# Router logits as columns of the output projection, and expert weights loaded in the last state-space block

## The reference

```python
h = tok(x)                                # patches -> LayerNorm -> W_proj -> LayerNorm, + positions
h = concatenate([h, txt(x_txt, ids)], 1)  # features of tokens -> LayerNorm -> gelu MLP
h = h + attn(layernorm(h))                # state-space block
h = h + ffn(layernorm(h))                 # mixture of 8 experts, one per token

def attn(x):                              # (32 sequences, 325 tokens, 192)
    xn = gamma * x / rms(x)
    xc = causal_conv4(xn @ W_in.T + b_in)             # 384 channels
    y  = scan(h = sigA * h + sigB * xc; y = h . sigC) # 16 states per channel
    return y @ W_out.T + b_out + x
def ffn(x):
    logits = x @ Ws + bs                  # 8 experts
    e = argmax(logits); p = max(softmax(logits))
    return (gelu(x @ W1[e] + b1[e]) @ W2[e] + b2[e]) * p
```

## Time and profile before

| what | us |
|---|---|
| median of 3 runs (lowest, highest) | 1399.47 (1394.68, 1400.88) |
| the profiled execution | 1397.25 |
| its span in the profile | 1395.5 |

### The profile page before, as it was taken

The page is one execution under the profiler, slowest core; times in us unless marked ns, Lnnn a source line. Parts: engine busy times, 40 slices in busy tenths (PEclk is TensorE's granted clock), DMA queues, the critical chain, the costliest instruction groups (busy, mean ns, idle before and its releaser), DMA issues. The chain is left out here.

```text
span 1395.5 us, 38297 instructions
## 1 busy us (share of the span) xinstructions
PE 1165.6 (84%) x11847; PEld 1099.6 (79%) x11847; DVE 808.4 (58%) x2553; ACT 690.4 (49%) x1544; POOL 389.3 (28%) x358
## 2 busy tenths in 40 slices
PE   0398993466579999999999679996699999999998
PEld 0398993244469898898898479985699999999998
DVE  0777977774752633633635547877456565655564
ACT  2265661255662332332233246654477777777775
POOL 6877000000200300300202105546233323333333
PEclk9999997576689998998999989998799999999999
DMA  8866412003510422322334489993111111111110
GB/s 186 183 99 146 105 36 66 26 0 99 233 26 2 105 67 79 79 82 72 71 96 100 122 252 293 304 286 100 54 47 43 46 41 44 46 45 43 45 43 24
DMA packets 166427, 133.83 MB, mean 96 GB/s; under 512 B 77989, under 2 KB 155932, under 8 KB 164704
## 3 DMA queue, kind: packets, MB, share of 16 engines
q1 hardware_dynamic: 152352, 112.22, 30.1%
q0 software_dynamic: 10384, 17.49, 4.0%
q10 hardware_dynamic: 3600, 3.01, 0.8%
HBM read 89.97 MB, written 43.53 MB: 96 GB/s over the span
## 5 line engine op out<-in xcount | busy, mean ns | idle before, releaser
L2126 POOL DMA_INDIRECT out_dram<-ob,oi x89 | 126.8, 1425 | 285.1 <-DVE ob L2180 279.9
L2236 PE MATMUL ph<-zt,wc 64*128 64x128 f32 x3204 | 197.8, 275 | 3.4 <-issue 1.6
L2236 PEld LDWEIGHTS ph<-zt,wc 64*128 64x128 f32 x3204 | 192.2, 189 | 6.8 <-issue 5.3
L2228 PE MATMUL py<-w2c,ht 64*128 64x192 f32 x2136 | 194.1, 327 | 1.1 <-DVE yb L2178 1.1
L1493 PE MATMUL pa<-wi,xn 96*85 (+3 forms) x2048 | 187.1, 247 | 2.9 <-POOL mc L1345 2.9
L1493 PEld LDWEIGHTS pa<-wi,xn 96*85 96x85 f32 (+1 forms) x2048 | 181.7, 156 | 4.1 <-POOL mc L1345 3.2
L2151 ACT ACTIVATE ht<-ph,bc 128x128 f32<-128x128 f32 x534 | 156.9, 371 | 48.5 <-PE ph L2236 48.5
L2228 PEld LDWEIGHTS py<-w2c,ht 64*128 64x128 f32 x2136 | 172.7, 187 | 1.5 <-issue 1.3
L1356 POOL TENSOR_TENSOR bd<-rr,mc 128x656 f32<-128x656 f32 x48 | 61.6, 1284 | 309.2 <-PE pb L1511 188.3
L1367 DVE COPY x<-pa 85x384 f32<-85x384 f32 x100 | 55.4, 554 | 147.2 <-PE pa L1493 147.2
L336 PE MATMUL ps_y<-wg,xt 128*112 128x192 f32 x672 | 123.0, 335 | 14.7 <-DVE yg L426 10.6
(11 more groups left out here) (318 smaller groups left out, 1964.9 us busy)
## 6 DMA issues: line engine op xcount, KB each, us to landing
y<-yd SPq DMA_DIRECT2D x41, 384.0 KB, 5.0
gp<-kd SPq DMA_DIRECT2D x48, 246.0 KB, 2.8
xg<-in_x SPq DMA_DIRECT2D x16, 588.0 KB
xr<-xs SPq DMA_DIRECT2D x89, 98.0 KB, 1.9
yd<-yt SPq DMA_DIRECT2D x56, 144.0 KB, 1.9
hb<-h SPq DMA_DIRECT2D x41, 192.0 KB, 5.9
yd<-yt SPq DMA_DIRECT2D x40, 192.0 KB, 2.1
xg<-in_x SPq DMA_DIRECT2D x48, 112.0 KB
```

The source lines that it names most:

```text
L2126: pool.indirect_dma_start(out, bass.IndirectOffsetOnAxis(ap=oi[j][:, 0:1], axis=0), ob[j][:], None, bounds_check=bound, oob_is_err=False). ...
L2228: m = pe.matmul(py[h][:], ht[j][r, k, :], w2c[j % 2][r, k, :], start=(k == 0), stop=(k == FC - 1))
L2236: return pe.matmul(ph[c % 4][:, c // 4, :], wc[j][r, f:f + 128], zt[j][r, part, :], start=start, stop=stop, skip_group_check=True)
```

## The change

- **Logits.** The router's weights, centred over the 192 features (`wsc`), are multiplied in the text stage with W_out and with its bias: 8 more columns of `wo` (200 instead of 192) and a row of `wi`. The projection then has 8 columns more and one more matmul per column, which adds bias and bias logits from one row of ones; the add of `bo` on DVE is gone, as are `turn`, `take` and `logits`. The residual's part of the logits is computed in `mix`: block 0's X units become H units with 104 columns, whose 8 logit columns go to `lgx`, and two L units transpose these into `lgh`; DVE scales `lgh` once and adds it per pair.
- **Expert weights.** Loaded by SP in the last block of `mix`, one expert behind each of the loads of g = 3 to 10, into the memory of `xn`, whose last use is over by then.
- **Buffers.** Four result banks and four row buffers. POOL, after the scatters of a group, waits for those of the group before.
- **Last group.** Ten columns in place of eight and two. The statistics of its columns 6 and 7 are not issued: `stats(LAST, FL, PG)` covers columns 8 and 9 only.
- **Images.** The last 8 stores move to the text stage's SP stream, and `root_y(g, 0, CUT)` behind the first of the last two `take`s.

```diff
@@ embed_images
             for g in range(NGRP):
+                hi = GRID if g + 1 < NGRP else CUT
+                sp.wait_ge(row_done, GRID * g + hi)
+                store_rows(sp, h0, keep, g, 0, hi)
...
-                if g + 1 == NGRP:
-                    root_y(g, 0, CUT)
                 for j in range(2):
                     take(g * GRID + GRID - 2 + j, j)
+                    if g + 1 == NGRP and j == 0:
+                        root_y(g, 0, CUT)
@@ embed_text, SP
+                sp.dma_start(wsc[:, n, :], io["L0_ffn_Ws"][n * HD:(n + 1) * HD, :]).then_inc(p_in, 16)
+            with nc.allow_non_contiguous_dma(reason="one value per partition"):
+                sp.dma_start(boc[:], io["L0_attn_b_out"].rearrange("(k p) -> p k", p=HD)).then_inc(p_in, 16)
+            sp.dma_start(wi[HD:HD + 1, 0, 0:D], io["L0_attn_b_out"].unsqueeze(0)).then_inc(p_in, 16)
+            store_rows(sp, dr["h0"], keep, NGRP - 1, CUT, GRID)
@@ embed_text, DVE
+            dve.wait_ge(p_turned, 1)
+            dve.scalar_tensor_tensor(out=wsc[:], in0=po[0][0:HD, 0, 0:NEX].unsqueeze(1).to_broadcast([HD, 2, NEX]),
+                                     scalar=-1.0 / D, in1=wsc[:], op0=ALU.mult, op1=ALU.add).then_inc(w2_ready, 1)
@@ embed_text, ACT
+                if m == 2:
+                    act.wait_ge(p_turned, 6)
+                    act.wait_ge(p_taken, 4)
+                    act.copy(wo[:, :, D:DX], po[1][:, 0, 0:KO * NEX].rearrange("p (k e) -> p k e", e=NEX))
+                    act.copy(wi[HD:HD + 1, 0, D:DX], po[1][HD:HD + 1, 1, 0:NEX]).then_inc(p_taken, 1)
+                    act.copy(wi[0:HD, :, EB:EB + NEX], wsc[:])
@@ embed_text, PE
+                if m == 2:
+                    pe.wait_ge(w2_ready, 1)
+                    for k in range(KO):
+                        for q in range(2):
+                            pe.matmul(po[1][:, 0, k * NEX:(k + 1) * NEX], wout_row[:, q, k * 128:(k + 1) * 128],
+                                      wsc[:, q, :], start=(q == 0), stop=(q == 1))
+                    for q in range(2):
+                        t = pe.matmul(po[1][0:HD + 1, 1, 0:NEX], boc[:, q:q + 1].to_broadcast([HD, HD + 1]), wsc[:, q, :],
+                                      start=(q == 0), stop=(q == 1))
+                    t.then_inc(p_turned, 1)
+                    pe.wait_ge(p_taken, 5)
@@ mix, SP
             def body(k, last):
                 for g in range(3, NG):
                     load(k, g, start(k) + 2 * (g - 2))
+                    if last and g - 3 < NEX:
+                        expert_weights(g - 3)
@@ mix, readers
+            if kind == "H":
+                flat = p[0:W, :, :].rearrange("w a b -> w (a b)")[:, 0:4 * (EB + NEX)].rearrange("w (c e) -> w e c", c=4)
+                copy(lgx[:, :, 4 * n:4 * n + 4], flat[:, EB:, :])
+                copy(x[:, :, 4 * n:4 * n + 4], flat[:, 0:EB, :]).then_inc(free[who], 1)
+            elif kind == "L":
+                copy(keep["lgh"][:, 4 * n:4 * n + 4, :], p[:, :, HALO:W]).then_inc(free[who], 1)
@@ mix, PE
             for m in range(XU):
-                input_unit(0, 0, m, m)
+                head_unit(m)
+            for n in range(LU):
+                p = bank(0, XU + n)
+                for who in range(2):
+                    pe.wait_ge(free[who], XU // 2 + 2)
+                for i in range(NEX // LU):
+                    tr = pe.transpose(p[:, i, 0:W], lgx[:, n * NEX // LU + i, :], ident[0:W, 0:W])
+                tr.then_inc(unit, 1)
@@ project_route, POOL
+            def group(g, a, half):
                 pool.wait_ge(rows_ok, g + 2)
                 hold(pool, tick_p)
+                scatter(a % NR, range(TG), a % 2)
+                if a:
+                    pool.wait_ge(sent[(a - 1) % 2], 16 * TG * (half + 1))
                     hold(pool, row_free)
@@ project_route, PE
             def project(p, g, q):
                 pe.wait_ge(y_in[q], 32 * (g + 1))
-                pe.wait_ge(h_done, p + 3)
+                pe.wait_ge(h_done, p + 1)
                 for i in range(2):
                     for k in range(KO):
+                        pe.matmul(po[q][:, i, 0:DX], yt[q][:, k, 1 - i, :], keep["wo"][:, k, :],
+                                  start=(k == 0), stop=False)
+                    m = pe.matmul(po[q][:, i, 0:DX], keep["ident"][0:HD + 1, HD:HD + 1].to_broadcast([HD + 1, CB]),
+                                  keep["wi"][0:HD + 1, 0, 0:DX], start=False, stop=True)
                 m.then_inc(out_ok, 1)
...
             def body(g, par, first):
                 for q in range(PG):
+                    project(PG * g + q, g, q)
                     if q == 2 and not first:
                         rank(g - 1, TG)
@@ project_route, DVE
                 dve.wait_ge(hb_ok, p + 1)
-                tt(hb[q][:], hb[q][:], bo[:, :].unsqueeze(1).to_broadcast([CB, 2, D]), ALU.add).then_inc(biased, 1)
-                dve.wait_ge(biased, p + 1)
                 dve.wait_ge(out_ok, p + 1)
...
+                tt(lgs[par][:, t:t + 2, :], po[q][:, :, D:DX], lgh[:, :, bass.ds(2 * p, 2)].rearrange("c e t -> c t e"),
+                   ALU.add)
+                tt(row[par][:, t:t + 2, 0:D], hb[q][:], po[q][:, :, 0:D], ALU.add).then_inc(h_done, 1)
...
+            dve.wait_ge(w_in, 32)
+            groups(dve, body, take_b1)
+            finish(NFULL, FL, 0, TG)
             c = Chain()
+            route1(LAST, FL, TL, stats(LAST, FL, PG), c)
+            route2(LAST, FL, TL, TG * LAST, mask10, c)
+            route3(LAST, FL, TL, TG * LAST, c)
```

More of the change, by code:

```diff
@@ L59 @@
 ROW = D + 4
+DX = D + NEX
 FAR = 1 << 20
@@ L854, in _ @@
             sums(0, HB)
-            pe.wait_ge(p_in, 80)
+            pe.wait_ge(p_in, 160)
+            for k in range(2):
+                t = pe.matmul(po[0][0:HD, 0, 0:NEX], keep["ones"][0:HD, 0:HD], wsc[:, k, :], start=(k == 0), stop=(k == 1))
+            t.then_inc(p_turned, 1)
             for k in range(2):
@@ L1226 @@
 XU = CB // 4
+LU = 2
 IU = EB // 4
@@ L1243, in unit_order, with mix @@
     return order
-def mix(nc, io, dr, keep, xn):
+def mix(nc, io, dr, keep, late, xn):
     with ExitStack() as ctx:
@@ L1493, in input_unit, with head_unit @@
                         mm = pe.matmul(p[:, i * EB:(i + 1) * EB], xn[0:rows, f, b, c * Q:c * Q + W],
-                                       keep["wi"][0:rows, f, bass.ds(k * EB, EB)],
+                                       keep["wi"][0:rows, f, bass.ds(k * EB + NEX, EB)],
                                        start=(f == 0), stop=(f == 1))
+                mm.then_inc(unit, 1)
+            def head_unit(m):
+                p = bank(0, m)[0:W, :, :].rearrange("w a b -> w (a b)")
+                for c in range(NCHUNK):
+                    for f in range(2):
+                        rows = HD + f
+                        mm = pe.matmul(p[:, c * (EB + NEX):(c + 1) * (EB + NEX)], xn[0:rows, f, m, c * Q:c * Q + W],
+                                       keep["wi"][0:rows, f, 0:EB + NEX], start=(f == 0), stop=(f == 1))
                 mm.then_inc(unit, 1)
@@ L1671, in project_route, with groups @@
         mu, rs = keep["mu"], keep["rs"]
-        w1, w2, b1, b2 = late["w1"], late["w2"], late["b1"], late["b2"]
-        def groups(eng, body):
+        b1, b2 = late["b1"], late["b2"]
+        def groups(eng, body, between=None):
             body(0, 0, True)
-            with eng.Fori(0, NFULL // 3) as i:
-                for a in range(1, 4):
-                    body(3 * i + a, a % 3, False)
+            if between:
+                between()
+            body(1, 1, False)
+            with eng.Fori(0, NFULL // NR) as i:
+                for a in range(2, 2 + NR):
+                    body(NR * i + a, a % NR, False)
         def empty_rows(eng, experts):
@@ L1793, in body @@
                     residual(g, q)
-                    if not (first and q == 0):
-                        take(PG * g + q - 1, (q - 1) % 2)
                     if not first and q == 0:
```

304 lines of the change are left out of this document (124 added, 180 removed).

## The result

The changed kernel takes 1435.54 us (median of 5, 1427.88 to 1436.55) against 1395.17 us for the kernel before on the same chip (median of 5, 1394.02 to 1400.88): ratio 1.0274, 95% interval 1.0249 to 1.0299. It is 2.7% slower. The forecast was 1401 us, with a range of 1387 to 1414.

What follows compares the result with a forecast made beforehand. Routing was taken as bound by a loop of DVE sums, PE's rank and projections (14.24 us a group), not PE alone. Terms summed to +2.4 us on 1397.25, giving 1399.7, or 1401.9 by the median; stated 1401, range 1387 to 1414.

Steps and rivals of the forecast that it cites:

- Images: Image stage: eight of SP's last 16 stores moved to the text stage, square root one copy later; -6.9 us.
- Text: Text stage: extra small matmuls, transfers and copies for the logit weights; +2.7 us.
- Inputs and L units: Inputs of block 0: records of 104 columns for 96, +3.4 us; two transpose units and a second drain, +2.0.
- Expert weights in the last block: Last state-space block: 9.44 MB between gp loads on SP's in-order queue delay gp; +14 us, bounds +10 and +25.
- rival 1: Last block starves: weights at 240 GB/s or below, block costs +25 us, total 1412; chance 0.25.
- in-order queue: Last block: assumed SP's one queue serves in order, so gp loads land behind weights issued before them; basis of +14 us.
- Routing, steady: Routing's eight steady periods: 13.9 us each for 14.83, PE's relief mostly becoming a wait at the rank; -7.5 us.
- Rival 3: Routing becomes PE-bound at 11.4 us a period: 20 us more off, total 1381; chance 0.10.
- Routing, start: Start of routing: PE's first projection no longer behind table load and centring, 4.3 us earlier; -4.0 us.
- End: End of routing: last group of ten columns, POOL ending 28.5 us behind the last full rank for 29.8; -1.3 us.
- Experts: Experts' stage: code untouched, taken at the same time; forecast called wrong if it changes by over 2 us.
- two terms of opposite sign: Largest loss and gain in the sum: expert weights in the last block +14 us, steady routing periods -7.5 us.

Runs made afterwards that it cites:

- w_long_pieces: Changed kernel with the same expert weight bytes in the same number of transfers but longer pieces (W2 4.6 KB for 768 bytes); 1430.3 us.
- w_on_gpsimd: Changed kernel with the 32 expert weight transfers issued by GpSimd in the last block instead of by SyncE between the gp loads; 1425.1 us.
- keep_pe_busy: Changed kernel with seven idle products (14 records) on PE ahead of each rank in the routing loop; median 1419.8 us.
- best3_busy_end: Changed kernel with rank and ACT's root later, weights spread over last block and routing, 36 idle products at routing's end; 1.0 to 1.1% faster than the kernel before.

## Why the prediction was wrong

*Images* -6.9: right, -8.7 and alone -8.2; the twelve profiles have -6.3 to -9.9. *Text* +2.7: +0.7, so the insertions cost less than I counted. *Inputs and L units* +5.4: +3.6, but with 3.1 us less at the low clock, worth 1.6. At full speed the records went from 83.5 to 90.1 ns, so the 6.7 ns counted were right (8/96 of 84.7 would be 7.1).

*Expert weights in the last block*, +14: this step failed, at +25.8. The place and the wait were those described, PE behind ACT behind a late gp, and the price was my upper bound (+25 at 240 GB/s), which was also rival 1's price. The wrong choice was the rate: I took 343 GB/s from two microseconds of y and hb loads and called 240 a mean of a stage. Measured were 242 with gp, 277 for weights alone. I looked for the cause in the small pieces; w_long_pieces excludes the weights' pieces. What remains is a cost of the engines per byte in this block: packets of 768 bytes take 47.5 ns on average there against 40.3 in routing before, the 328-byte ones of gp 31.7 ns against 22.4 in the block before. Why they are slower wasn't tried and stays open. The in-order queue on which the sum stood wasn't decisive: gp was late with no weights ahead of it on its queue too (w_on_gpsimd). And I counted no loss of clock; over the stretch it is 0.82.

The 436 GB/s of the Trainium skill ("DMA: Bandwidth & Descriptors", anatomy of one DMA), which I weighed against the rows, would have given half of this term, an estimate; the page states the figure for transfers that GpSimd issues. The measured rate is 242, and 268 with the weights issued by GpSimd.

*Routing, steady*, -7.5: this is the second and larger error, 16.8 us and in the sign too, +9.3. The loop was right: PE's wait of "about 2.5 us a group" is 2.7, and the period at full clock is 14.33 for the forecast 13.9 (DVE's part 7.57 for 7.33, with 1.37 us of waiting for ACT in it, and the two projections with the sum behind them 6.04 for 5.85). What failed is the sentence that makes PE's relief "a wait at the rank" and stops there, with no price on the wait. Here it wasn't free: in six of eight periods the clock fell to 1.2 GHz in it or just behind it, and what PE does next lies on the loop. It cost 8 x (15.99 - 14.33) = 13.3 us, of which 0.6 are the fifth period's own; keep_pe_busy gave 13.0 back over the eight. The rows of before held a warning: waits of 0.6 to 1.5 us at the rank, one low stretch in eight periods and clocks below 1 in the stretches with waits. The rest of the miss is 8 x (14.33 - 13.9) = 3.4 us. No rival had the clock in it; rival 1's total of 1412 was too low for that reason, although its block was right.

Rival 3, PE-bound at 11.4 us, was judged rightly: "the rank keeps its place in PE's order" is what kept it away. Moving it one projection gives 11.5 to 12.1 us in six of eight periods, and 11.3 with ACT's root moved too.

*Routing, start* -4.0: -1.8. PE's first projection stands 6.1 us behind the stage's first load where it was 9.9, so these 4 us came; it waits for hb by DMA (10.5 us idle, the barrier in it) and not for its tables. Two of them were lost again ahead of the first rank, in which PE waits 1.0 us for hb and 2.15 at the rank. *End* -1.3: -0.5, with the last rows ready at 994.86, 14.8 us behind the last full rank, as forecast. *Experts* 0: +3.4, against the 2 us allowed. The low clock lasts 3.3 us longer in the stage (14.8 for 11.5 us), which is worth 1.7. The rest is open; it isn't chance, since all twelve profiles with the changed routing and buffers have 412.4 to 417.2, and the two without 410.8 and 412.2.

The sum was near zero because two terms of opposite sign stood against each other. Both missed in the same direction.

## What to carry to other kernels

Work taken off an engine that waits elsewhere becomes idle time, and idle time of TensorE has a price if what follows it is on the loop. Where a relief turns into a wait, ask at once whether the waiting instruction can stand one step later in the engine's order: here that one line was worth 23 to 29 us, three to four times the planned gain. And before bytes are moved under a stage "with idle queues", divide them by the slowest rate that the trace shows for such loads and compare that with the idle DMA time: 9.44 MB at 242 to 277 GB/s are 34 to 39 us, and all that was idle in 60 us of the block were 35.

## What was not expected of the hardware

- Useless work made the kernel faster: 14 records on PE in each wait took 12.7 us off routing in the pair of profiles, and the median from 1435.5 to 1419.8.
- The time SP takes to issue a transfer isn't fixed. It was 0.5 us for `lg`, 2.5 to 2.7 with weights on the queue, and 6.9 and 9.98 us with the weights on another queue.
- A busy share of the DMA engines near 1 says nothing of the rate: 0.93 went with 296 GB/s, 1.07 with 268 and 277, 1.11 with 242.
- Work ahead of a barrier didn't save the clock behind it. In best3_busy_end PE worked for 14.2 us, then waited 4.9 us across the barrier, and the clock was low for 13.7 us from 962.3 on.
- A second queue can make a small load later. With the weights on GpSimd's queue, a gp took 22.5 us to land for 2.8 us in the kernel before.
